# A graph layer's gathers wait for the batch four ahead of them instead of the batch seven ahead

## The reference

```
theta = x[dst] - x[src]
w     = sigmoid(relu(theta @ W1 + b1) @ W2 + b2)
agg   = segment_sum(w * theta, dst);  indeg = segment_sum(1, dst)
out   = layernorm(x + agg + indeg * (x @ W4 + b4))
```

## Time and profile before

| what | us |
|---|---|
| median of three runs | 5248.88 |
| lowest and highest run | 5244.53, 5276.63 |
| span of the profiled execution | 5257.5 |
| TensorE matmul busy | 4021.0 (76%) |
| GpSimd busy | 3071.6 (58%) |
| VectorE busy | 2289.7 (44%) |
| ScalarE busy | 1222.0 (23%) |
| mean granted TensorE clock | 0.842 of 2.4 GHz |

### The profile page before, as it was taken

The page is one execution under the profiler, slowest core; times in us unless marked ns, Lnnn a source line. Parts: engine busy times, 40 slices in busy tenths (PEclk is TensorE's granted clock), DMA queues, the critical chain, the costliest instruction groups (busy, mean ns, idle before and its releaser), DMA issues.

```text
span 5257.5 us, 79790 instructions
## 1 busy us (share of the span) xinstructions
PE 4021.0 (76%) x23554; PEld 2973.8 (57%) x23956; DVE 2289.7 (44%) x9032; ACT 1222.0 (23%) x2536; POOL 3071.6 (58%) x3231
## 2 busy tenths in 40 slices
PE   6777877777778777777777777777777877777776
PEld 4555555555556555555555555555555555555555
DVE  3444444444444444444444444444444444444444
ACT  2222222222222222222222222222222222222222
POOL 5555555556555655655565555655555565655554
PEclk8888888888888888888888887888888888888888
DMA  1111111111111111111111111111111111111111
GB/s 45 44 44 44 45 44 45 44 44 45 43 45 44 45 44 43 45 45 45 43 45 44 43 43 43 45 44 44 44 44 43 44 45 44 45 44 45 45 43 34
DMA packets 187593, 230.45 MB, mean 44 GB/s; under 512 B 105912, under 2 KB 136012, under 8 KB 187572
## 3 DMA queue, kind: packets, MB, share of 16 engines
q0 software_dynamic: 103296, 211.41, 15.5%
q1 hardware_dynamic: 84276, 18.80, 1.7%
HBM read 222.36 MB, written 7.60 MB: 44 GB/s over the span
## 4 chain that ended last, share of the span: by engine, by line
PE 53%; another core or an unknown queue 29%; issue 10%; ACT 6%; DVE 1%; SPq 0%; ACTq 0%; DMA 0%; DVEq 0%
PE ps_hid L399 15%; PE ps_log L407 11%; PE ps_sum L421 10%; PE ps_hid L382 7%; PE ps_srcT L391 5%; ACT hidden L486 3%; PE ps_rel L371 3%; ACT srcT L480 3%; PE ps_win L435 1%; ACT wgt L493 1%; PE ps_sum L415 0%; PE ps_win L429 0%; DVE hot_en L593 0%; ACTq L83 0%
## 5 line engine op out<-in xcount | busy, mean ns | idle before, releaser
L357 POOL DMA_INDIRECT gath<-in_x,src_i x3224 | 3070.9, 953 | 2145.3 <-remote 890.9
L593 DVE SCALAR_TENSOR_TENSOR hot_en<-col_no,rel,wgt 128x128 f32<-128x128 f32 x3224 | 920.2, 347 | 2025.7 <-ACT wgt L493 1498.1
L399 PE MATMUL ps_hid<-srcT,neg_w 128*128 128x512 f32 x1612 | 1081.2, 760 | 663.6 <-ACT srcT L480 421.1
L407 PE MATMUL ps_log<-w,hidden 128*128 128x1 f32 x6448 | 861.0, 255 | 416.2 <-ACT hidden L486 400.9
L407 PEld LDWEIGHTS ps_log<-w,hidden 128*128 128x128 f32 x6448 | 865.4, 209 | 473.8 <-issue 357.2
L421 PE MATMUL ps_sum<-gath,hot_en 128*128 128x129 f32 x6448 | 1015.8, 307 | 0.0
L584 DVE TENSOR_SCALAR_CACHE_REDUCE hot_ne<-ps_rel,row_no 128x512 bf16<-128x512 f32 x806 | 604.4, 750 | 781.7 <-remote 402.3
L486 ACT ACTIVATE hidden<-ps_hid,b_col 128x512 f32<-128x512 f32 x806 | 553.8, 687 | 1564.7 <-PE ps_hid L399 1028.9
L421 PEld LDWEIGHTS ps_sum<-gath,hot_en 128*128 128x128 f32 x6448 | 897.9, 215 | 0.0
L480 ACT COPY srcT<-ps_srcT 128x512 f32<-128x512 f32 x806 | 471.0, 584 | 1568.1 <-remote 1051.8
L399 PEld LDWEIGHTS ps_hid<-srcT,neg_w 128*128 128x128 f32 x1612 | 303.4, 235 | 704.3 <-ACT srcT L480 442.2
(11 more groups left out here) (67 smaller groups left out, 1015.7 us busy)
## 6 DMA issues: line engine op xcount, KB each, us to landing
gath<-in_x,src_i POOLq DMA_INDIRECT x3224
window<-in_x SPq DMA_DIRECT2D x116, 64.0 KB
out<-yout SPq DMA_DIRECT2D x116, 64.0 KB
first_i<-in_dst SPq DMA_DIRECT2D x116, 0.5 KB
src_i<-in_src SPq DMA_DIRECT2D x115, 14.0 KB
dst_i<-in_dst SPq DMA_DIRECT2D x115, 14.0 KB
w<-in_L_gnn_W SPq DMA_DIRECT2D x2, 64.0 KB
b_rows<-in_L_gnn_b SPq DMA_DIRECT2D x1, 64.0 KB
```

Of the source, the lines that this page charges most:

```text
L357: nc.gpsimd.indirect_dma_start(gath[0:parts, t, 0:F], None, x, bass.IndirectOffsetOnAxis(ap=src_i[0:parts, k.parity, t:t + 1], axis=0))\
L399: nc.tensor.matmul(ps_hid[b][:, :], neg_w1[:, :], srcT[:, b, :], start=False, stop=True)\
L407: last = nc.tensor.matmul(ps_log[:, t:t + 1], hidden[:, b, t * P:(t + 1) * P], w2[:, :], start=True, stop=True)
L593: last = nc.vector.scalar_tensor_tensor(hot_en[:, b, t, :], col_no[:, :], rel[:, k.parity, e:e + 1], wgt[:, b, t:t + 1].to_broadcast([P, P ...
```

## The change

A constant `HELD = 3` is added to what the gathers of a batch wait for. The batch at place i in the whole order waited for the add_up of batch i-7; now it waits for the add_up of batch i-4. Nothing else is touched: the same gathers, in the same order, into the same slots.

```
+HELD = 3
...
                 for j in range(batches):
                     if not is_first(k):
-                        pool.wait_ge(summed, (k.c - 1) * NB + j + 1)
+                        pool.wait_ge(summed, (k.c - 1) * NB + j + 1 + HELD)
                         pool.sem_inc(pool_gate, 1)
```

## The result

The changed kernel took 5266.68 us (median of 20 runs, 5243.62 to 5290.08) against 5247.51 us for the kernel before (20 runs): a ratio of 1.0033, 95% interval 1.0018 to 1.0048. I had forecast 5380 us and a range from 5225 to 5600; measured is a seventh of the loss forecast. It later turned out that the comparison depends on where it runs. Six further jobs ran on six different chips. On two of them the kernel before takes 5248 and 5258 us, on the other four 4101 to 4113 us. The first result is of the slow kind, in which before takes about 5250 us.

What follows compares the result with a forecast made beforehand. The prediction held that no engine filled the span and that others learning late of TensorE's work cost time. To the median of 5249 us it added 130 us for late transposes: 5380 us, range 5225 to 5600, chance 0.50.

Steps and rivals of the forecast that it cites:

- Nothing added, only the gathers' start moves: On all engines: no instruction added or removed, the constant costs no time; only when a batch's four gathers may start moves.
- The latency of 6.69 us: From the end of the add_up that frees a batch's slots to its gathered data landing: 0.82 + 5.87 us.
- the leads of under 6.7 us: From the end of the add_up four ahead to a batch's transposes: 393 of 802 too short, median 6.8 us.
- gross sum of 401 to 468 us: At the transposes: all lateness moved on batch by batch, 401 us over 363 batches, 468 with the 0.30 us hand-over.
- The sum: At the transposes: lateness over 802 batches, counting only what exceeds the late start of ScalarE's copy; about 130 us lost.
- late copy: ScalarE's copy starting much later than its transposes end; transposes up to that much later were to cost nothing.
- net sum of 128 us: At the transposes: lateness beyond the copy's late start, 87 us over 168 batches, 128 with the 0.30 us hand-over.
- Hidden after all: Rival, at the transposes: lateness vanishes behind late news or in evener steps; under 52 us lost, about 5265 us; chance 0.24.
- late news: Other engines learn late that TensorE has finished; ScalarE's copy waits 1051.8 us in 196 waits for an unnamed releaser.
- All of it counts: Rival, on TensorE: late transposes also delay logits and add_up, or lower the clock; 5650 to 5720 us; chance 0.14.
- Faster: Rival, on GpSimd: pauses break runs of eight gathers, halving hidden_src's 442.2 us of waits for copies; 5158 us; chance 0.12.
- What bounds the kernel: Whole kernel: no engine fills the span; gathers bound nothing by latency, others learning late of TensorE's work costs time.

Runs made afterwards that it cites:

- three_ahead: The kernel before with its gathers waiting for the add_up three batches ahead instead of seven: 9502.18 us against 4101.61, ratio 2.316.
- five_ahead: The kernel before with its gathers waiting for the add_up five batches ahead instead of seven: 4102.13 us against 4101.61, ratio 1.000.

## Why the prediction was wrong, point by point

- **Nothing added, only the gathers' start moves**: right. GpSimd's busy time is 3069.2 us against 3071.6.
- **The latency of 6.69 us and the leads of under 6.7 us**: right. I counted 363 late batches; 395 waits for a gather are in the trace. From the end of a batch's last gather to its transposes my sum has 1.48 us, and the shortest in the trace of after is 1.49. The sign "1 to 7 us ahead of their transposes" came true as well (1.5 to 6.9 us). The waits cost 624.8 us of idle TensorE, more than the gross sum of 401 to 468 us.
- **The sum**: this step failed. I let each loss shift all that follows and looked for cover in one place only, the late copy of the same batch. That left a net sum of 128 us. Measured are 17 to 19 us. What the runs showed in its place: TensorE already stood idle for 1236.5 us, 1.5 us a batch, and still does (1199.5 us). 681.4 us ahead of the transposes took the place of 661 us of later waiting ahead of hidden_src and the logits. The trace of before held the sign of it. There 410 batches' transposes begin less than 6.99 us (6.69 and the 0.30) behind the news of the add_up that frees their gathers, and taken one by one they fall short by 589 us. TensorE sat idle for 2.5 us in the mean in the step behind each of them and for 0.4 us behind the others; 476 of the 589 us would lie within the idle time of the same step. The leads had come from TensorE's own rows; I should have asked where TensorE itself waits next behind each late transposition. The 400.9 us of waits for the relu, directly behind the transposes in its order, were in the answer that I had, and I used them nowhere.
- **Hidden after all**: this rival came out (0.24). Its sign, no waits at the transposes, did not: the waits are there and cost nothing in total. Both of its reasons are in the trace in part. Lateness goes along with late news (149 of the 157 late copies), against my argument that short steps have no idle time to take it. And steps did become more even (386 under 5 us, now 157). What I had named too narrowly is where the cover lies: also in the wait for the relu.
- **All of it counts**: false on this kind of chip, although its sign came true: over 350 waits at the transposes. Its mechanism, the lower clock, is real one step further: three_ahead ran at 0.65 and lost 2.1 us more per batch than my sum for the chain at 2.4 GHz. With four ahead the mean over the span hides it (0.847 against 0.842), but the add_ups were busy 57.4 us longer, more of them at the lower level. I had weighed only the mean clock. The Trainium skill's "TensorE: Matmul & The Clock Gate", section "HAM oscillation — how this bites in real kernels", says that a TensorE left waiting for data begins its next work cold. three_ahead agrees with it: behind the wait of 3.71 us the transposes took 1.00 us, against 0.60 in the earlier trace rows.
- **Faster**: copies over 2 us late did fall from 1179 to 660 us, and the total did not. Runs of eight gathers were hardly broken up, 234 before and 222 after by the trace, so the lever of this rival wasn't there. That the copies are less late because the wait moved ahead of their transposes fits the counts and wasn't tested.
- **What bounds the kernel**: "gathers bound nothing by their latency" held only for the chip I saw. And "the trace can't name it" deserved an experiment before it deserved a place in a sum: it is the gathers. The Trainium skill's "SBUF — State Buffer", section "🔬 SBUF: two separate sides", says that TensorE waits for nobody at its ports. Leaving out half the gathers took TensorE's batch from 6.5 to 4.1 us, which shows that gathers cost it time on this kind of chip; no run shows that they do it at those ports, so page and measurement can both hold.

Shown is that TensorE's new waits cost it no idle time in total, and that gathers cause the late news on one kind of chip. That new waits lie inside old ones is argued from the totals, the counts and the two places in the timeline; a true loss that is made up by more even steps would leave the same totals and isn't excluded. The last 0.3% stands in busier add_ups; why they ran slower is argued only. Open are: what makes chips or jobs differ, how dense gathers must be, and whether it is bytes or GpSimd's work.

## What to carry to other kernels

A new wait on the busiest engine need not be a loss where that engine has a later wait that it can stand in for. Before pricing it, add up the engine's idle time by what ended it, and see how much of it stands behind the new wait. Then read the busy time of its groups too, as a wait may come back as slower work. If the idle time of every engine has a cause that the profile can't name, find that cause by leaving work out before pricing a change. And measure a change of slack on more than one chip: the same edit was 0.3% here and 2.0% there, because another engine was the bound.

## What the runs showed of the hardware

- The same program took 5248 to 5258 us on some chips and 4101 to 4113 us on others, each within 0.6% of its median, at granted clocks of 0.84 and 0.98. By the traces other engines learn late of TensorE's finished work on the former (247 copies over 2 us late) and never on the latter. Half the gathers remove it (3326 us against 5258). The ends of TensorE's rows are modelled, so the traces don't tell late news from matmuls that end later than their rows say.
- One indirect gather of 128 rows costs GpSimd 0.95 us and 0.30 us of gap whether a row has 512 or 256 bytes (4101 and 4122 us for the whole kernel).
- An instruction of 0.37 us between two gathers costs 0.23 us, as it lies partly in their gap.
- TensorE ran at a mean granted clock of 0.655 in three_ahead, where it was idle for 3516 of 9502 us, and at 0.985 in five_ahead, where it was idle for 650 of 4103 us.
- In the changed kernel 38% of the add_ups' matmuls began at the lower level of the clock in steps whose transposes had waited, and 6% in the others. The mean time of all of them rose from 307 to 319 ns.
